# A gated attention and mixture-of-experts kernel: x1 and the normed rows of B and C on VectorE, and all engines' steps in another order

## What is computed

```
x = x + tanh(g_xattn[0]) * layernorm(x) * R        # R: decayed running sum (0.9) of ctx*ctx over the sequence
x = x + tanh(g_ffn[0])   * ffn0(layernorm(x))      # x W^T plus a low-rank adapter of 4, the likeliest one only
x = x + tanh(g_xattn[1]) * attn(layernorm(x), ctx) # 16 heads of 16, sigmoid in place of softmax
x = x + tanh(g_ffn[1])   * moe(layernorm(x))       # 8 experts, 2 per token, gelu, 256 -> 256 -> 256
```

## Time and profile before

| what | value |
|---|---|
| span of the profiled execution | 478.9 us |
| median of the runs less the span | 7.9 us |
| PE busy | 396.5 us (83%) |
| VectorE busy | 370.2 us (77%), 1416 instructions |
| ScalarE busy | 330.9 us (69%), 671 instructions |
| POOL busy | 251.4 us (53%), 313 instructions |
| mean granted TensorE clock | 0.961 of full |
| long pauses on POOL | 39, 28.7 us |
| short pauses on POOL | 32, 10.9 us |

### The profile page before, as it was taken

The page is one execution under the profiler, slowest core; times in us unless marked ns, Lnnn a source line. Parts: engine busy times, 40 slices in busy tenths (PEclk is TensorE's granted clock), DMA queues, the critical chain, the costliest instruction groups (busy, mean ns, idle before and its releaser), DMA issues.

```text
span 478.9 us, 13099 instructions
## 1 busy us (share of the span) xinstructions
PE 396.5 (83%) x4092; PEld 309.2 (65%) x4092; DVE 370.2 (77%) x1416; ACT 330.9 (69%) x671; POOL 251.4 (53%) x313
## 2 busy tenths in 40 slices
PE   2758899998999989998899887789568898989950
PEld 1446667776776777676677765478457797777740
DVE  2788888998988889898888785368556566789993
ACT  2755788898889889998888775576616564655640
POOL 1621212545553464637453556678876676766760
PEclk9988999999999999999999999889969999999995
DMA  7336686664575555876454665525353559397975
GB/s 231 90 111 178 181 215 177 183 194 133 166 227 182 162 174 161 244 178 209 144 170 125 220 189 146 166 67 151 90 157 103 165 162 335 101 351 244 330 262 201
DMA packets 69501, 87.12 MB, mean 182 GB/s; under 512 B 9485, under 2 KB 55290, under 8 KB 69306
## 3 DMA queue, kind: packets, MB, share of 16 engines
q1 hardware_dynamic: 60074, 65.81, 47.4%
q0 software_dynamic: 6816, 18.65, 10.5%
q10 hardware_dynamic: 2544, 1.81, 1.2%
HBM read 51.07 MB, written 35.18 MB: 180 GB/s over the span
## 4 chain that ended last, share of the span: by engine, by line
PE 46%; DVE 14%; issue 13%; POOL 11%; ACT 8%; DMA 6%; another core or an unknown queue 1%; ACTq 1%; DVEq 0%; POOLq 0%; SPq 0%
PE ps_J L1654 13%; PE ps_F L1654 6%; PE ps_O L1768 5%; PE ps_T L1663 5%; PE ps_S L1755 4%; POOL store_x L765 4%; POOL pause_t L782 3%; PE ps_S L1654 3%; DMA store_y<-y_out,y_row 2%; POOL store_y L771 2%; PE ps_R L1693 2%; DVE y_out L2938 2%; PE ps_O L1779 2%; PE ps_G L1654 2%; DMA temp_t<-in_temp 2%
## 5 line engine op out<-in xcount | busy, mean ns | idle before, releaser
L771 POOL DMA_INDIRECT store_y<-y_out,y_row x78 | 78.4, 1005 | 41.6 <-DVE y_out L2938 29.5
L765 POOL DMA_INDIRECT store_x<-xn_E,slot_u x64 | 68.8, 1076 | 27.1 <-DVE slot_u L2637 16.9
L1093 ACT ACTIVATE prob<-ps_S 128x512 f32<-128x512 f32 x128 | 72.4, 594 | 12.0 <-PE ps_S L1755 7.6
L1755 PE MATMUL ps_S<-q_stack,k_stack 128*128 128x256 f16 x256 | 44.5, 276 | 5.6 <-issue 3.5
L2926 DVE TENSOR_TENSOR h_lo<-h_f,h_hi 128x512 f16<-128x512 f32 x39 | 26.9, 689 | 24.5 <-ACT h_hi L1177 19.6
L1654 PE MATMUL ps_J<-wout_hi,h_hi 128*128 x112 | 31.2, 278 | 15.2 <-DVE y_out L2938 12.9
L1768 PE MATMUL ps_O<-prob,v_wide 128*32 128x128 f32 x1024 | 41.0, 279 | 1.1 <-ACT prob L1093 0.9
L1169 ACT ACTIVATE h_f<-ps_F,bin_t 128x256 f32<-128x256 f32 x56 | 23.5, 471 | 25.9 <-PE ps_F L1654 20.1
L1654 PE MATMUL ps_F<-xb_hi,win_hi 128*128 128x256 f16 x112 | 31.8, 284 | 4.1 <-DVE xb_lo L2907 2.7
L1779 PE MATMUL ps_O<-wo_t,av 128*128 128x256 f32 x128 | 32.8, 401 | 2.3 <-ACT av L1121 1.6
L751 POOL TENSOR_TENSOR rstd_C<-var_C,minus_half 128x2 f32<-128x2 f32 x16 | 12.2, 761 | 40.3 <-DVE var_C L2416 40.3
(11 more groups left out here) (302 smaller groups left out, 1410.6 us busy)
## 6 DMA issues: line engine op xcount, KB each, us to landing
parts_scratch<-parts SPq DMA_DIRECT2D x32, 256.0 KB
k_stack<-parts_scratch SPq DMA_DIRECT2D x64, 128.0 KB
q_stack<-parts_scratch SPq DMA_DIRECT2D x128, 64.0 KB
xb<-store_x SPq DMA_DIRECT2D x30, 257.0 KB
y_got<-store_y SPq DMA_DIRECT2D x14, 512.0 KB
c_in<-in_ctx SPq DMA_DIRECT2D x16, 256.0 KB
x_in<-in_x SPq DMA_DIRECT2D x16, 256.0 KB
store_x<-zeros SPq DMA_DIRECT2D x15, 257.0 KB, 4.8
```

The source lines that it names most:

```text
L765: pool.indirect_dma_start(store_x, bass.IndirectOffsetOnAxis(slot_u[q][:, at:at + 1], 0), xn_e[q][:, at, :], None).then_inc(s_scat[q], 16)
L771: pool.indirect_dma_start(store_y, bass.IndirectOffsetOnAxis(y_row[n][:, b:b + 1], 0), y_out[n][:, b, :], None).then_inc(s_y_kept[n], 16)
L1093: act.activation(prob[m % PROBS][:, 2 * n:2 * n + 2, :, :], bank_s[n], ACT.Sigmoid, scale=float(HD) ** -0.5).then_inc(s_prob[n], 1)
L1755: ins = pe.matmul(bank_s[n][:, g % 2, :, :], k_stack[q][:, g, k, cut], q_stack[q][:, :, g, k, cut], start=True, stop=True)
```

## The change

1. ScalarE's `gained`, `normed_b` and `normed_c` go: six instructions of 256 columns per pair. `shifts_a` and the `shifts` of B and C go from VectorE. `normed_e` and the shift of E stay.
2. `moves` is now (x - mean) * R and `make_x1` is moved * ln_gain + x, each two instructions of 256 columns (scalar_tensor_tensor) where there was one of 512 columns (tensor_tensor). `moves` no longer waits for ScalarE or for the power, only for the means and for R; `make_x1` waits for the gain, and for x2 of the pair two before.
3. `normed_b` and `normed_c` are now VectorE steps, two tensor_scalar instructions of 256 columns each, with two scalars read per partition.
4. The order of the steps is another one on all five queues, and the loops of the expert phase and of the outputs are written out too, with an order of their own. No other step is added or taken away: the 39 long and 32 short pauses are all there, at other places, six of the short ones behind the last `keep_block`.

The core of the diff, with the stretches of the lists that matter most:

```
-            def shifts_a(p):
-                dve.scalar_tensor_tensor(out=shift["A"][q][:, :], in0=mv["A"][q][:, :, 0], scalar=-1.0,
-                                         in1=ln_gain[q][:, :], op0=ALU.mult, op1=ALU.mult).then_inc(s_shift["A"], 1)
-            def moves(p):
+            def moves(p):
                 dve.wait_ge(s_scan, p + 1)
-                dve.wait_ge(s_xn["A"], 2 * p + 2)
-                need(dve, s_x1, p)
-                dve.tensor_tensor(moved[:, :, :], x1[p % 2][:, :, :], bank_r, ALU.mult).then_inc(s_moved, 1)
+                dve.wait_ge(s_aggr["A"], 2 * p + 2)
+                need(dve, s_x1, 2 * p)
+                for b in range(2):
+                    dve.scalar_tensor_tensor(out=moved[:, b, :], in0=x_in[q][:, b, :], scalar=mv["A"][q][:, b, 0:1],
+                                             in1=bank_r[:, b, :], op0=ALU.subtract, op1=ALU.mult).then_inc(s_moved, 1)
             def make_x1(p):
-                dve.wait_ge(s_moved, p + 1)
-                dve.tensor_tensor(x1[q][:, :, :], moved[:, :, :], x_in[q][:, :, :], ALU.add).then_inc(s_x1, 1)
+                dve.wait_ge(s_moved, 2 * p + 2)
+                dve.wait_ge(s_gain, p + 1)
+                need(dve, s_x2, p - 1)
+                for b in range(2):
+                    dve.scalar_tensor_tensor(out=x1[q][:, b, :], in0=moved[:, b, :], scalar=ln_gain[q][:, b:b + 1],
+                                             in1=x_in[q][:, b, :], op0=ALU.mult, op1=ALU.add).then_inc(s_x1, 1)
+            def normed(k, p, src):
+                dve.wait_ge(s_rstd[k], p + 1)
+                need(dve, s_t[k], p)
+                for b in range(2):
+                    dve.tensor_scalar(xn[k][:, b, :], src(b), mv[k][p % 2][:, b, 0:1], rstd[k][p % 2][:, b:b + 1],
+                                      ALU.subtract, ALU.mult).then_inc(s_xn[k], 1)
...
```

More of the change, by code:

```diff
@@ L3817, in _ @@
             adapter_picked(15)
+            next(early)
             adapter_sum(15)
@@ L3822, in _ @@
             adapter_gated(15)
-            next(early)
             down_hi(15)
@@ L3985, in _ @@
-            for n in range(TILES + 1 - ADD_AT, NP):
-                add_pair(n)
+            take_rows(8)
+            add_bias(8)
+            take_rows(9)
+            hidden_lo(9)
+            slots(15)
+            next(final)
+            next(final)
+            copy_lo(11)
+            next(final)
+            next(final)
+            add_bias(9)
+            hidden_lo(10)
+            copy_lo(12)
+            next(final)
+            next(final)
+            next(final)
+            next(final)
@@ new lines, in _ @@
+            next(final)
+            take_rows(10)
+            add_bias(10)
+            hidden_lo(11)
+            copy_lo(13)
+            take_rows(11)
+            add_bias(11)
+            next(final)
+            take_rows(12)
+            hidden_lo(12)
+            copy_lo(14)
+            add_bias(12)
+            hidden_lo(13)
+            copy_lo(15)
+            take_rows(13)
+            hidden_lo(14)
+            add_bias(13)
+            copy_lo(16)
+            copy_lo(17)
+            take_rows(14)
@@ new lines, in _ @@
+            copy_lo(22)
+            add_bias(19)
+            hidden_lo(20)
+            next(gates)
+            next(gates)
+            take_rows(20)
+            next(gates)
+            next(gates)
+            hidden_lo(21)
+            take_rows(21)
+            take_rows(22)
+            take_rows(23)
+            copy_lo(23)
+            add_bias(20)
+            copy_lo(24)
+            hidden_lo(22)
+            add_bias(21)
+            add_bias(22)
+            next(gates)
+            hidden_lo(23)
@@ new lines, in _ @@
+            copy_lo(25)
+            next(gates)
+            copy_lo(26)
+            hidden_lo(24)
+            take_rows(24)
+            take_rows(25)
+            add_bias(23)
+            hidden_lo(25)
+            take_rows(26)
+            take_rows(27)
+            copy_lo(27)
+            next(gates)
+            add_bias(24)
+            hidden_lo(26)
+            add_bias(25)
+            take_rows(28)
+            copy_lo(28)
+            next(gates)
+            add_bias(26)
+            hidden_lo(27)
@@ new lines, in _ @@
+            copy_lo(29)
+            add_pair(0)
+            hidden_lo(28)
+            add_bias(27)
+            copy_lo(30)
+            add_pair(1)
+            add_pair(2)
+            take_rows(29)
+            hidden_lo(29)
+            copy_lo(31)
+            add_bias(28)
+            add_pair(3)
+            hidden_lo(30)
+            copy_lo(32)
+            add_bias(29)
+            copy_lo(33)
+            hidden_lo(31)
+            add_pair(4)
+            take_rows(30)
+            add_bias(30)
@@ new lines, in _ @@
+            hidden_lo(32)
+            copy_lo(34)
+            take_rows(31)
+            add_bias(31)
+            add_pair(5)
+            hidden_lo(33)
+            take_rows(32)
+            take_rows(33)
+            copy_lo(35)
+            add_bias(32)
+            hidden_lo(34)
+            copy_lo(36)
+            add_bias(33)
+            add_pair(6)
+            hidden_lo(35)
+            take_rows(34)
+            take_rows(35)
+            add_bias(34)
+            copy_lo(37)
+            add_pair(7)
@@ L3989 @@
+            hidden_lo(36)
+            add_bias(35)
+            copy_lo(38)
+            take_rows(36)
+            add_bias(36)
+            hidden_lo(37)
+            add_pair(8)
+            take_rows(37)
+            take_rows(38)
+            add_bias(37)
+            hidden_lo(38)
+            add_pair(9)
+            add_bias(38)
+            add_pair(10)
+            add_pair(11)
+            add_pair(12)
+            add_pair(13)
+            add_pair(14)
+            add_pair(15)
 KINDS = ("k_hi", "k_lo", "q_hi", "q_lo")
```

2253 lines of the change are left out of this document (1289 added, 964 removed).

## The result

The changed kernel took 507.56 us (median of 4, 502.99 to 510.27) against 486.31 us (4 runs, 483.74 to 487.15): ratio 1.044, 95% interval 1.0378 to 1.0503. Ratios and intervals in this document compare the quick executions of two kernels, so where some executions of a set were slow a ratio is not the quotient of the two medians, which are of all. The profiled execution took 508.32 us with a span of 506.4 us, so only 1.9 us lie around the span; over all executions on record it is 1.8 to 3.0 us. So the 7.9 us that I had carried as a constant came from setting the span of one execution of before beside the median of others.

A forecast was written before the change was run, and what follows sets the result against it. No engine plainly bound the pair phase, though VectorE's list was about fullest; a POOL-caused stall and VectorE bound the tiles. Terms -1 -1 -10 -2 -2 = -16 took 486.8 to 471 us, range 458 to 488.

The forecast's parts named there:

- POOL at the first tiles: First output tiles: fewer pauses between indirect DMAs remove the 11.8 us take_rows(8) stall; -10 us (-13 to 0).
- pair phase: 62 to 280 us: VectorE becomes fullest at 15.85 us a pair, 16.7 with idle time; -1 us over 14 pairs.
- tiles 8 to 27: Output tiles: transposes and copies up to two tiles ahead fill some of PE's waiting; -2 us (+2 to -7).
- pauses were of use: Rival, chance 0.17: indirect DMAs without pauses slow down or delay tile loads, so the -10 becomes 0 to -3; 480 us.
- price of tensor_scalar: VectorE's normed_b and normed_c: 0.34 us per 256-column instruction, 0.26 of the queue, 1.04 us a pair.
- idle time of 0.85 us a pair: Pair phase: of VectorE's 2.11 us idle a pair, 0.85 stays as waits for ScalarE and ffn0 shrink.
- VectorE overfull: Rival, chance 0.16: new tensor_scalar wait for POOL instructions in the pair phase, 18.0 us a pair; 490 us.
- the start: Kernel start: the first running sum begins before the gates land, power chains lose a ScalarE hop; -1 us (+2 to -3).
- Moved steps: Steps placed behind others, such as slots(15) behind hidden_lo(9): loads still early enough, no cost counted.
- cover of load_block(16): Near tiles 12 to 15: load after pair 15's last scatter has two tiles' time; if not, 3 to 5 us once.
- tail: Last tiles: ten add_pair instead of twelve ahead of the last add_bias on VectorE; -2 us (0 to -3).

The follow-up runs named there:

- after_again: The changed kernel run again unaltered in set 3, which had no late signals: 1.6% faster than the kernel before.
- before_x1: Kernel before with only x1 made on VectorE in two steps of two 256-column instructions, no shift of A, no ScalarE step for x1: ratio 1.002.
- the spaced kernels: Changed kernel with long pauses added between neighbouring indirect DMAs: everywhere (102 more) 524.8 us, in the pair phase alone (31 more) 500.45 us.
- the three spacings of set 4: Kernel before with take_rows late from tile 8 on, and no, short or long pauses on POOL: 493.0, 482.6 and 479.2 us.
- before_normed: Kernel before with only the normed rows of B and C as four tensor_scalar a pair on VectorE, at the places of their shifts: ratio 1.024.
- The five kernels above: before_x1, before_normed, after_again, the kernel before with a useless VectorE load (1.036), and the kernel before without pauses (2.1% faster).
- before_late_rows: Kernel before with take_rows of tiles 8 and on moved right ahead of add_bias of the same tile, every pause kept: ratio 0.983 in set 3.
- after_tile_pauses: Changed kernel with spaced scatters in the pair phase and about the kernel before's spacing in the tiles, in set 2 without late signals: ratio 1.037.
- the first after: The changed kernel in its first measurement, against the kernel before, with late signals: 507.56 us, ratio 1.044.
- the late rows alone: Kernel before with only take_rows from tile 8 on moved right ahead of its add_bias: 0.983 in set 3, 0.999 in set 4.
- The two together: Kernel before with take_rows late from tile 8 on and all POOL pauses left out, in set 4 with late signals: 493.0 us, 1.021.
- sets 2 and 4: Groups of runs on one chip each beside the kernel before: set 2 priced the VectorE edit's halves, set 4 varied pauses with late take_rows.

## Why the prediction was wrong, step by step

**POOL at the first tiles (-10 us), and the step that failed.** The term was right in mechanism and size without late signals: tiles 0 to 8 take 28.0 us in after_again against 39.1 in before_x1, which has before's POOL list and VectorE order there. In the first measurement it still gave 5.9 us. What failed is the price of taking pauses from between indirect DMAs: I counted it in POOL's own time alone and put its effect on the other engines at nothing, in this term, in the pair phase (-1) and in tiles 8 to 27 (-2), as if an indirect DMA could only be late itself. What the runs show in its place are PE's signals, held back 1 to 7 us. The pair phase came to +15.8 us for -1, tiles 8 to 27 to +14.7 for -2, and to tile 38 another +6.8. Set against the same kernel without late signals, the pair takes 17.97 - 16.94 = 1.03 us more (13 us over 13 pairs), and tiles 0 to 38 take 159.6 us in place of 129.6. This is a difference between two sets; the spaced kernels and the three spacings of set 4 tie it to the signals, within a set. Against the kernel before, which has late signals too (484 and 482 us with, 469 without), the change of sign from 0.984 to 1.044 is 6% or 28 us.

**The rival "pauses were of use" (0.17, 480 us)** was the right one, with the wrong price: I let it take the -10 back, but not go beyond. My own line that "something must have shown them good" deserved a bound from the waits of before, where the three remote rows stood to be read.

**Pair phase (-1 us).** The price of tensor_scalar was low: beside nothing on POOL it takes 407 ns (400 in before_normed), not 340, 0.27 us a pair too little. Other terms were high by more, for VectorE works 15.5 us a pair and not 15.85. The Trainium skill, "VectorE: DVE Perf Modes", in "Mode 2×_2P", had it at two results a cycle; my estimate from that page was 290 ns by that and 423 ns by one, and the trace agrees with the slower one. Without late signals the error is the idle time of 0.85 us a pair that I left VectorE. The five kernels above keep 1.42 to 1.75. In after_again it is 15.52 us of work (199.75 / 218 x 16.94) and 1.42 idle, 16.94 a pair, against 16.49 in before_late_rows: +6 us over 13 pairs where I had -1.

**VectorE overfull (0.16, 490 us)** gave 18.0 us a pair and 17.97 came, by luck. Its mechanism, tensor_scalar held by POOL, is real but small: 476 ns on average beside an indirect DMA (7 instructions of B), 406 beside a power. Only a memset held it for long, once a kernel (2.75 us in the changed one), at the start, for which my sum had nothing; that may be why the start gave 0.0 and -0.5 us for my -1. The Trainium skill, "SBUF — State Buffer", in "SBUF: two separate sides", has a VectorE instruction in a two-port mode and a GpSimd one lock each other out; the memset agrees, with 3.64 us, while the powers, by which I had weighed that rule, did not hold a tensor_scalar. Whether the new tensor_scalar ran in such a mode is not shown.

**Moved steps.** The cover of load_block(16) held in after_again and was gone in after_tile_pauses, for 9.6 us where I had 3 to 5. In the first after, SP's load of tile 16 waited instead for the last step of the final plan (3.2 us), which stood on VectorE at 385.61, behind the 6.2 us of tile 10: a late signal passed on.

**Tiles 8 to 27 (-2) and tail (-2).** 65.8 us in after_again against 61.4 in before_x1, so +4.4: steps further ahead filled nothing, and PE waits up to 1.9 us for a load that SP issues later. The last eleven tiles took 35.8 against 36.7, 3.25 us a tile, near the forecast 3.2, and the end behind them 2.4 us more (464.0 - 447.1 against 467.8 - 453.3), so the two pairs put there were probably not free.

**The sum without late signals**, profiled after_again against profiled before_x1 (which is level with before): up to make_x2 of pair 2 0.0, pairs +5.0, from there to tile 0 -3.6, first tiles -11.1, tiles 8 to 27 +4.4, to tile 38 -0.9, end +2.4, in all -3.8 (spans 464.0 and 467.8; that is -0.8%, of a profiled execution 3.9 us over its median; the timed runs give -1.6%). I had forecast -3.3%. That the first tiles gained what I had said and the rest lost a part of it leaves the right sign here; it is not the measurement that I had forecast.

**A version better than both.** Without late signals, the kernel before without pauses: 459.84 us, 0.979. With late signals nothing beat the kernel before; the late rows alone are level with it there (0.999) and 0.983 without, so of the changes made in both kinds of set they are the one that never lost. The two together ran only with late signals (1.021).

**Open.** What makes a set show late signals. The results of sets 2 and 4 name the same chip number, one set without them, one with. All executions of a set go together in time, but each of them has a span and a clock on record, so none is known to have run without records being taken. With 18 to 25% of the semaphore records missing just where signals are late, it stays possible that the taking of records holds the signals, or that one cause lies behind both; no run tells these apart, and a kernel timed with nothing recorded would. Which part of an indirect DMA holds PE's signal was not separated either. Both states were not seen on one chip within a set.

## What to carry to other kernels

A step that does nothing but keep other steps apart (a pause on POOL) can be paid back on an engine that the step never touches: before it is taken out, read the waits for rows whose releaser is no engine, in the kernel that still has it. The engine with the fullest list kept some idle time whatever it was given here (1.4 us or more of 17), and of the work added to it two thirds to three quarters were paid, so idle time should not be counted on to take it. And a kernel whose median differs by 3% between sets has two regimes: compare inside a set, and look which regime it is, by the remote waits and by the number of semaphore records, before a theory is built on it.

## What the runs showed of the hardware that I had not expected

- PE's signals came up to 7 us behind the recorded end of their product when three or more indirect DMAs of POOL stood 1.27 us apart (63 to 88% of the signals late), never without an indirect DMA (0 of 655), and in three of six sets only. In the traces of these three 18 to 25% of the semaphore records are missing (8465 for 11281 in the same kernel); cause and effect are not separated.
- With pauses of 0.73 us between the indirect DMAs the late signals of the changed kernel fell from 62 to 3. Short pauses of 0.2 us, which leave them 1.29 to 1.48 us apart, did not prevent one of 7.5 us.
- A tensor_scalar of 256 columns between SBUF tiles took 0.407 us, and 3.64 us when POOL's memsets ran beside it; a tensor_tensor power on POOL did not lengthen it (0.406 us).
